# An attention block on one core: the loop over sequence pairs of the attention stage written out as sixteen steps

## What is computed

```python
x = x + _layernorm(_L0_attn_ref(_layernorm(x), Wq, Wk, Wv, Wo, betas, memory0, z0))
x = x + _layernorm(_L0_ffn_ref(_layernorm(x), cn_*, gc_*, adaptive_range))

# _L0_attn_ref, for each of the 4 segments in turn (H = 16 heads of 64):
scores = where(mask, -inf, q @ k.T * scale)
att_dot = softmax(scores) @ v
sq = elu(q) + 1.0
att_mem = sq @ M / (sq @ Z.T)
sk = elu(k) + 1.0
M, Z = M + sk.T @ v, Z + sk.sum(rows)
att = gate * att_mem + (1.0 - gate) * att_dot
out = att.reshape(B, LSEG, H * DV) @ Wo

# _L0_ffn_ref: a small net of the sequence's mean, then three cycles of
tf = coupling_net(out)                      # four layers, gelu and sigmoid
out = out + (BASE + adaptive_range * (0.7 * gf + 0.3 * tf - 0.5) * 2.0) * twist(out)
```

## Time and profile before

| | us |
|---|---|
| median of 3 runs | 1248.91 |
| lowest, highest | 1248.09, 1250.15 |
| profiled execution, its own time | 1248.27 |
| span of the profiled execution | 1246.5 |

### The profile page before, as it was taken

The page is one execution under the profiler, slowest core; times in us unless marked ns, Lnnn a source line. Parts: engine busy times, 40 slices in busy tenths (PEclk is TensorE's granted clock), DMA queues, the critical chain, the costliest instruction groups (busy, mean ns, idle before and its releaser), DMA issues.

```text
span 1246.5 us, 20616 instructions
## 1 busy us (share of the span) xinstructions
PE 1066.8 (86%) x7108; PEld 745.9 (60%) x7172; DVE 823.6 (66%) x1492; ACT 611.5 (49%) x1291; POOL 586.0 (47%) x715
## 2 busy tenths in 40 slices
PE   2898989887999898879999988898998879999972
PEld 1476767664767676647676766676767665433331
DVE  3868686865686868656867686768686652444375
ACT  3545454544454544544535445445454553566663
POOL 2145454554454545544545454545454551323266
PEclk9999999988999999989999999999999888999995
DMA  6100000000000000000000000000000010300014
GB/s 156 30 10 9 10 9 10 10 11 10 10 9 10 9 10 10 10 11 10 9 9 9 10 10 10 9 10 9 9 1 9 2 28 1 144 0 0 1 34 102
DMA packets 14954, 24.02 MB, mean 19 GB/s; under 512 B 5376, under 2 KB 7168, under 8 KB 14336
## 3 DMA queue, kind: packets, MB, share of 16 engines
q1 hardware_dynamic: 14848, 22.63, 6.3%
HBM read 13.97 MB, written 8.65 MB: 18 GB/s over the span
## 4 chain that ended last, share of the span: by engine, by line
PE 43%; DVE 31%; issue 11%; ACT 10%; POOL 2%; DMA 2%; DVEq 0%; SPq 0%; POOLq 0%; ACTq 0%
PE ps L1216 10%; DVE arena L816 9%; PE ps L1111 8%; PE ps L1329 6%; ACT arena L576 4%; PE ps L1169 4%; PE ps L1342 3%; PE ps L1156 3%; DVE arena L760 3%; DVE arena L847 2%; PE ps L1174 2%; DVE arena L865 2%; DVE arena L826 2%; DVE arena L830 2%; DVE arena L837 2%
## 5 line engine op out<-in xcount | busy, mean ns | idle before, releaser
L1111 PE MATMUL ps<-arena 128*128 128x512 f16 x1152 | 272.7, 388 | 8.2 <-DVE arena L792 5.4
L576 ACT ACTIVATE arena<-ps,arena 128x128 f32<-128x128 f32 x512 | 139.3, 383 | 226.6 <-DVE arena L837 226.3
L816 DVE STREAM_TRANSPOSE arena<-ps 128x1024 f32<-128x1024 f32 x96 | 190.3, 1985 | 42.1 <-PE ps L1111 42.1
L1111 PEld LDWEIGHTS ps<-arena 128*128 128x128 f16 x1152 | 113.3, 100 | 133.5 <-issue 19.1
L420 POOL TENSOR_TENSOR arena<-arena 128x256 f32<-128x256 f32 x128 | 93.1, 728 | 131.2 <-DVE arena L847 131.1
L1169 PEld LDWEIGHTS ps<-arena 128*128 128x128 f32 x1024 | 133.0, 198 | 29.1 <-issue 20.6
L1169 PE MATMUL ps<-arena 128*128 128x65 f32 x1024 | 136.6, 278 | 15.5 <-DVE arena L847 14.3
L404 POOL TENSOR_TENSOR arena<-arena 128x512 f32<-128x512 f32 x64 | 81.4, 1271 | 124.4 <-ACT arena L569 124.4
L1216 PE MATMUL ps<-arena 128*128 128x256 f32 x544 | 122.0, 382 | 0.3 <-ACT arena L588 0.3
L390 POOL TENSOR_TENSOR arena<-arena 128x2 f32<-128x2 f32 x50 | 9.8, 197 | 238.0 <-DVE arena L756 238.0
L1216 PEld LDWEIGHTS ps<-arena 128*128 128x128 f32 x544 | 102.0, 190 | 16.1 <-ACT arena L588 1.4
(11 more groups left out here) (109 smaller groups left out, 1813.1 us busy)
## 6 DMA issues: line engine op xcount, KB each, us to landing
x_rows<-arena SPq DMA_DIRECT2D x17, 256.0 KB, 2.0
arena<-in_L_attn_x_dram SPq DMA_DIRECT2D x64, 64.0 KB
arena<-x_rows SPq DMA_DIRECT2D x4, 1024.0 KB, 8.1
out_dram<-arena SPq DMA_DIRECT2D x32, 128.0 KB, 2.8
arena<-in_L_attn_Wq_dram SPq DMA_DIRECT2D x1, 1024.0 KB, 13.8
arena<-in_L_attn_Wk_dram SPq DMA_DIRECT2D x1, 1024.0 KB, 18.9
arena<-in_L_attn_Wv_dram SPq DMA_DIRECT2D x1, 1024.0 KB, 22.5
arena<-in_L_attn_Wo_dram SPq DMA_DIRECT2D x8, 128.0 KB, 10.4
```

The source lines that it names most:

```text
L576: last = act.activation(Pr[:, par, j, :], s_bank[:, par, j * P:(j + 1) * P], ACT.Exp, bias=negm[:, par, j:j + 1])
L816: dve.transpose(dst[:, d0:d0 + 32, :], bank.rearrange("p w (d c) -> p d w c", c=C)).then_inc(x_free, 1)
L1111: last = pe.matmul(bank[:, w, :], xc[:, lx, k, w * P:(w + 1) * P], W16[lw][:, k, i, :], start=(n == 0), stop=(n == 5))
```

## The change

On GpSimd, ScalarE, VectorE and TensorE the loop over the first three pairs and the fourth pair written out become one loop of the generating program, `for bp in range(PAIRS)`, so that sixteen steps stand one behind the other in each engine's program. `bp` is then a number everywhere and all waits of the steps are on constants. The conditions for the last steps are given over the step's number instead of over s: `m < NT - 2` and `m == NT - 1`, which is the same as before in each of the sixteen. SyncE's program keeps its loop and is the same, instruction for instruction. What each step does, its order and its tiles are not changed.

```diff
@@ pool
-                with pool.Fori(0, PAIRS - 1) as bp:
+                for bp in range(PAIRS):
                     for s in range(NSEG):
-                        step(bp, s)
-                for s in range(NSEG):
-                    step(PAIRS - 1, s, s < NSEG - 2)
+                        step(bp, s, bp * NSEG + s < NT - 2)
@@ act, and word for word the same on dve and pe
-                with act.Fori(0, PAIRS - 1) as bp:
+                for bp in range(PAIRS):
                     for s in range(NSEG):
-                        step(bp, s)
-                for s in range(NSEG):
-                    step(PAIRS - 1, s, s < NSEG - 2, s == NSEG - 1)
+                        m = bp * NSEG + s
+                        step(bp, s, m < NT - 2, m == NT - 1)
```

More of the change, by code:

```diff
@@ L980, in _ @@
                 take_x(0, 0, 5, first=True)
-                with dve.Fori(0, PAIRS - 1) as bp:
+                for bp in range(PAIRS):
                     for s in range(NSEG):
-                        step(bp, s)
-                for s in range(NSEG):
-                    step(PAIRS - 1, s, s < NSEG - 2, s == NSEG - 1)
+                        m = bp * NSEG + s
+                        step(bp, s, m < NT - 2, m == NT - 1)
                 def couple(half):
@@ L1276, in _ @@
                 pe.wait_ge(c_in, 192)
-                with pe.Fori(0, PAIRS - 1) as bp:
+                for bp in range(PAIRS):
                     for s in range(NSEG):
-                        step(bp, s)
-                for s in range(NSEG):
-                    step(PAIRS - 1, s, s < NSEG - 2, s == NSEG - 1)
+                        m = bp * NSEG + s
+                        step(bp, s, m < NT - 2, m == NT - 1)
                 def net(half, layer):
```

## The result

The changed kernel takes 1229.9 us (median of 4, 1227.7 to 1230.9) against 1248.6 of the kernel before; the ratio is 0.984, with a 95% interval of 0.981 to 0.986. Run once more beside other kernels it took 1227.5 us, 0.982 (0.979 to 0.985). The forecast was 1236.3 us and a range of 1232.5 to 1239.8.

What follows compares the result with a forecast made beforehand. TensorE, busy 86% of the span, was taken to bound the kernel, standing at two loop jumps. Terms -13.56 + 0 + 0 + 1.0 = -12.6 us gave 1235.7 us profiled, 1236.3 us as median, range 1232.5 to 1239.8.

Steps and rivals of the forecast that it cites:

- TensorE's standing: At the loop's two jumps back between pairs, TensorE stands 5.76 and 5.73 us; straight code gives back 11.05 us.
- rival A: At pair boundaries the standing belongs to the place, not the jump; time stays 1248.9 us; chance 0.03.
- rival B: Instruction supply fails in straight code, 2.9 us late in each of twelve steps; 1271 us, slower; chance 0.03.
- The share of "issue" in the chain: Sign in the new trace: time waiting for nothing the profile shows, 11% of the last-ending chain, falls about one point.
- The crossings' clock: Behind the two jumps, the low clock after the standing goes too: 2.5 us of the 13.56 us saved.
- The waits on constants: In the steps, register instructions ahead of waits are hidden behind the engines' queues: 0 us, at most 0.1 for twelve steps.
- The other engines' jumps: At the jumps back, ScalarE's 1.59 us is covered and VectorE jumps while waiting for TensorE; removal earns nothing.
- The clock in the inner steps: In the eleven steps within pairs, low-clock stretches shift once the stalls go: +1.0 us, between -4.3 and +3.3.
- the end that I called its most: Rival where the clock takes back its most: inner steps all at 61.5, +3.3 us; 1240.0 us in all; chance 0.16.
- start and rest: Before 69.90 us the same work; from 937.77 us to the end 0, with 0.7 us either side, twice.

Runs made afterwards that it cites:

- e2: Kernel before with TensorE's sixteen steps alone written out, the other engines keeping their loops: 1243.84 us, ratio to before 0.995.
- e3: Kernel before with VectorE's steps alone written out, TensorE keeping its jumps: 1243.0 us, ratio to before 0.995.
- e7: Changed kernel, but VectorE alone keeps the real loop with its registers and two jumps: 1238.0 us, ratio to before 0.991.
- e8: Changed kernel, but ScalarE and GpSimd keep their loops, TensorE and VectorE straight: 1228.35 us, ratio to before 0.983.
- e10: Kernel before, loops and all, with extra unread matmuls in TensorE's longest idle place of each step: 1248.87 us, ratio to before 0.998.
- e4: Changed kernel with extra unread matmuls, 8 or 12, in TensorE's longest idle place of each step: 1224.83 us, ratio to before 0.980.
- e9: The changed kernel itself, run once more beside other kernels for a second profile: 1227.5 us, ratio to before 0.982.
- e11: Changed kernel with unread matmuls in idle places, plus 4 more in the last step of each of the first three pairs: 1222.17 us, ratio to before 0.976.
- e1: Changed kernel with the first three pairs in three one-trip loops on the four engines, no branch taken backward: 1229.95 us, ratio to before 0.984.

## Why the prediction was right in kind and wrong in size

**TensorE's standing: right.** The term was 11.05 us of standing at two jumps, and the three crossings now go through without a gap. That the branch was the cause, and not the place (rival A), is shown by the crossings of the changed kernel and by e2. No engine near the path stood in the middle of straight code for 3 us on "issue" (rival B fell). The share of "issue" in the chain, which should have fallen by one point, fell by six: the chain takes another way through the steps now, and the standing was only part of what it counted, so that share was a poor measure.

What TensorE stood for can be followed in the instruction queue q8, which counts 63 transfers where TensorE has its loop (before, e3) and 57 where it is straight (the change, e2, e7, e8). Two of its 16 KB transfers start within the first standing, at 294.67 and 298.29 us; the queue's lines for 294 to 297 and for 297 to 301 us:

```profile
q8 instruction: 1, 0.02, 2.8%
q8 instruction: 1, 0.02, 2.0%
```

They end at 296.02 and 299.58; the two weight loads follow 1.9 us behind the first end, the matmul 1.3 us behind the second. It is so at all six jumps of before, e3 and e10 (1.8 to 1.9 and 1.2 to 1.4 us), and at the first crossing of the changed kernel no transfer of this queue falls between 286 and 298 us. At its second crossing one starts at 533.48 us, and nobody stands. By the Trainium skill, "Runtime: NRT & Kernel Launch", section Instruction fetch mechanics, a taken branch out of what is held waits for a fetch; the traces agree in these times, though no run changed the fetch by itself.

**The crossings' clock: the term was too small.** I took the exit as what a crossing will be: 20.03 us behind the last matmul. It is 18.90, at full clock. The exit had a low stretch of its own inside that window (0.93 on average, as the prediction itself noted) and I carried it over to all three; e10 shows the same exit without it at 18.96. 13.56 became 16.98 us, a miss of 3.4 (3 x 1.13).

**The waits on constants: this step failed.** The prediction put them at 0 us, since 61.50 us with registers and 61.49 with constants stood at the same mean granted clock of 0.97. The same mean doesn't make the same step: it says how long the low stretch is, not which work it falls on. In the earlier trace rows a three-step sum at 0.97 stood beside single steps that, in the same trace, run from 61.03 to 61.54 us at 0.97; in the changed kernel it is 60.66 to 61.70. Only steps at 1.00 could be compared, and the written-out end of the kernel before had none; there the answer was not in the windows but in the group of L847, 13.1 us of idle time that no other engine ended. The runs show 0.53 us a step (e10 against e4, e2 within one execution, e7), 4.8 us in the nine inner steps, and 0.45 to 0.65 in each crossing. And they are not hidden behind the engines' queues, as the prediction had it: in `divide` the register instruction waits for the reciprocal itself.

**The other engines' jumps: right for ScalarE and GpSimd, wrong for VectorE.** Removed together, as the change does, none is late, so the sum was not hurt. But the reason given, that VectorE jumps while it waits for TensorE, held only as long as TensorE stood: with TensorE straight, e2 shows 1.4 and 1.5 us of VectorE's jump on the path.

**The clock in the inner steps: right in sign, too small.** Forecast +1.0 us, between +3.3 and -4.3; it was +4.2 in the profiled execution, once the registers' 4.8 are taken out, so the end that I called its most was passed; the sum of the inner steps doesn't show it because the two cancel. In e9, the same program, the inner steps take 670.44 us and the clock's part is +2.0, so some 2 us of this term change from one execution to the next. That the low stretches go with TensorE's idle places is shown by e4 and e11, where they are gone once these are filled; which steps they fall on is not forecast by anything here, and e9 has them elsewhere.

Sum of the misses, for the profiled executions: forecast -12.6, crossings' clock -3.4, crossings before the last matmul -1.4, inner steps -0.5 instead of +1.0, start and rest -1.6: -20.5 of the -20.6 between the profiled executions; by the medians, -18.7, the forecast missed 6.4 us. The range was too narrow because both of its ends were made of the clock alone; the term held to be certain, 0 to 0.1 us for the registers, was off by some 6 us.

## What to carry to other kernels

Compare two stretches only at full clock, or look at where in them the low stretch falls: a mean granted clock that is equal is no proof of equal conditions. Where an instruction waits for the one just ahead of it on its own engine, look in the program for a register instruction between them: here each was on the path in full. Idle time of a group that no engine ended is where it shows. Working the value out ahead of the reciprocal should save the same without writing the loop out; no run tried it. And a stall that covers others hides their price: straighten all the engines that are near the path, or the next one takes over.

## What the runs showed of the hardware

- A jump back in TensorE's program held it for 5.10 to 5.76 us at six crossings (before, e3, e10), with two weight loads let through about halfway and two 16 KB transfers of the instruction queue q8 in that time; the same in VectorE's held it for 1.40 to 1.49 us (e2, e7), in ScalarE's for 1.55 to 1.86 (before, e2, e3, e8, e10). A loop end that is passed cost nothing measurable (e1 against the changed kernel).
- A register instruction between two dependent instructions of VectorE cost 0.09 us (gaps of 0.129 against 0.040 us).
- Matmuls that nobody reads, 8 or 12 in a step, kept TensorE's granted clock at 1.00 through eleven inner steps, seven of which had a low stretch at 0.50 in the profile of the changed kernel, and with 4 more at each crossing made the kernel faster by 5 to 8 us (1222.2 against 1227.5 and 1229.9). In the kernel with jumps they gained nothing clear (1248.9, 0.997 to 1.000).
